# The row maximum of the combine weights, taken from the stored logits or from the reloaded ones

## What is computed

```
x = layernorm(x) ;  se = layernorm(slot_embeds) * scale
logits   = einsum('bnd,esd->bnes', x, se)                    # 2048 rows x 1024 slots
dispatch = softmax(logits, axis=1)                           # over the 1024 rows of a batch
combine  = softmax(logits.reshape(B, N, -1), axis=-1)        # over the 1024 slots of a row
slots = einsum('bnd,bnes->besd', x, dispatch)
gate  = gelu(slots @ Wg + bg) ;  up = slots @ Wu + bu
eout  = (gate * up) @ Wd + bd
out   = einsum('bns,bso->bno', combine, eout)
```

## Time and profile before

| | us |
|---|---|
| median of 3 runs | 626.82 (626.4 to 627.47) |
| the profiled execution | 631.37 |
| its span | 629.6 |
| PE busy | 572.9 (91% of the span) |
| DVE busy | 481.6 (76%) |
| ACT busy | 394.8 (63%) |
| POOL busy | 323.8 (51%) |

### The profile page before, as it was taken

How to read it: one execution, slowest core, us unless ns; L and a number is a source line. 1 busy time by engine, 2 the same in 40 slices (tenths; PEclk the granted TensorE clock), 3 DMA queues, 4 the chain that set the end, 5 groups by cost and what they waited for, 6 DMA issues and landing times.

```text
span 629.6 us, 11863 instructions
## 1 busy us (share of the span) xinstructions
PE 572.9 (91%) x3888; PEld 511.8 (81%) x3888; DVE 481.6 (76%) x1335; ACT 394.8 (63%) x1054; POOL 323.8 (51%) x324
## 2 busy tenths in 40 slices
PE   7697999999979999899888985999879999979998
PEld 3577999999979999899876764988747777769998
DVE  3666877787886978886757998898797999964553
ACT  3747959596864859587734535466465666564563
POOL 5817344444444444443438968666066999830000
PEclk9888999999998999999999999899988999998999
DMA  7800000000020000000002433050057888703552
GB/s 237 219 2 1 2 2 2 1 2 1 10 76 2 2 2 1 2 2 2 1 2 100 169 131 135 1 199 8 1 186 248 266 267 268 269 33 118 176 169 75
DMA packets 34828, 53.36 MB, mean 85 GB/s; under 512 B 6125, under 2 KB 21425, under 8 KB 34769
## 3 DMA queue, kind: packets, MB, share of 16 engines
q1 hardware_dynamic: 34769, 52.61, 24.8%
HBM read 42.12 MB, written 10.49 MB: 84 GB/s over the span
## 4 chain that ended last, share of the span: by engine, by line
PE 50%; DVE 20%; ACT 16%; issue 8%; POOL 5%; DMA 0%; DVEq 0%; SPq 0%; POOLq 0%; ACTq 0%
ACT expo L671 8%; PE ps L1236 8%; PE ps L1367 8%; PE ps L1322 6%; PE ps L1297 5%; PE ps L1344 4%; DVE expo L901 3%; PE ps L1268 3%; DVE qT_low L795 2%; PE ps L1171 2%; PE ps L1356 2%; ACT pT_high L685 2%; PE ps L1190 2%; DVE wkq_low L1016 2%; PE ps L1149 2%
## 5 line engine op out<-in xcount | busy, mean ns | idle before, releaser
L671 ACT ACTIVATE expo<-expo,nmin 128x154 f32<-128x154 f32 x256 | 106.2, 418 | 63.6 <-DVE nmin L901 62.9
L537 POOL TENSOR_TENSOR prob<-expo,prec 128x512 f32<-128x512 f32 x64 | 67.1, 1048 | 113.7 <-DVE prec L912 113.5
L921 DVE TENSOR_TENSOR pT_low<-ps,pT_high 128x512 fp32r<-128x512 f32 (+1 forms) x96 | 54.3, 591 | 19.4 <-ACT pT_high L685 19.2
L901 DVE CUSTOM_DVE_ANT_0 expo<-ps,maskb 128x154 f32<-128x154 f32 x256 | 66.9, 311 | 0.0
L1190 PE MATMUL ps<-kbd,qT_high 128*128 128x308 f32 x256 | 60.7, 322 | 6.0 <-DVE nmin L901 5.7
L598 POOL TENSOR_TENSOR wkq_low<-w_raw,wkq_high 128x1024 fp32r<-128x1024 f32 x16 | 50.8, 3180 | 27.2 <-ACT wkq_high L629 27.2
L685 ACT CAST pT_high<-ps 128x512 fp32r<-128x512 f32 (+1 forms) x96 | 45.9, 512 | 6.1 <-PE ps L1202 5.9
L808 DVE TENSOR_TENSOR w_gu_low<-w_raw,w_gu_high 128x1024 fp32r<-128x1024 f32 x18 | 45.4, 2533 | 4.4 <-ACT w_gu_high L629 4.2
L671 ACT ACTIVATION_READ_ACCUMULATOR expo<-expo,nmin 128x1 f32 x256 | 48.5, 189 | 0.0
L1190 PEld LDWEIGHTS ps<-kbd,qT_high 128*128 128x128 f32 x256 | 40.2, 190 | 9.7 <-DVE nmin L901 9.4
L795 DVE SCALAR_TENSOR_TENSOR qT_low<-ps,bq_c,qT_high 128x256 fp32r<-128x256 f32 x64 | 30.7, 480 | 15.9 <-ACT qT_high L607 15.8
(11 more groups left out here) (215 smaller groups left out, 1824.3 us busy)
## 6 DMA issues: line engine op xcount, KB each, us to landing
logits_dram<-lsb SPq DMA_DIRECT2D x16, 512.0 KB, 2.6
w_raw<-in_L_ffn_Wg_dram SPq DMA_DIRECT2D x16, 512.0 KB, 4.2
w_raw<-in_L_ffn_Wu_dram SPq DMA_DIRECT2D x16, 512.0 KB, 4.5
w_raw<-in_L_ffn_Wd_dram SPq DMA_DIRECT2D x16, 512.0 KB, 4.3
lraw<-logits_dram SPq DMA_DIRECT2D x16, 512.0 KB, 3.5
out_dram<-outb SPq DMA_DIRECT2D x16, 128.0 KB, 1.7
x<-in_x_dram SPq DMA_DIRECT2D x1, 1792.0 KB, 10.1
wraw<-in_L_xattn_Wk_dram SPq DMA_DIRECT2D x2, 512.0 KB, 5.7
```

What stands on the lines that cost most here:

```text
L537: pool.tensor_tensor(prob[:, n % 2, :, heads, :], expo[:, n % 2, pp, :, :, 0:P], prec[:, n % 2, pp].unsqueeze(3).to_broadcast([P, 2, 2, P] ...
L671: ins = act.activation(row, row, ACT.Exp, scale=-1.0, bias=nmin[:, n % 2, pp, j, h:h + 1], accum_out=psums[:, n % 2, pp, j, h:h + 1])
L901: ins = dve.tensor_tensor_reduce(out=expo[:, n % 2, pp, j, h, :], in0=ps[:, s % NS, h * SK:(h + 1) * SK], in1=maskb[:, (2 * (n // QUADS) + ...
L921: dve.tensor_tensor(pT[1][0:rows, n % 2, 2 * t:2 * t + tiles], ps[0:rows, NS + k % NT, 0:tiles * 2 * P].rearrange("p (t n) -> p t n", t=ti ...
```

## The change

The 16 row maxima leave the logits and slots stages. Each is taken in the combine stage instead, by the same DVE instruction, from the reloaded tile `lraw[:, i % 3]` in place of `lsb[:, i]`. DVE now waits for the load, and ACT's exponential waits for the maximum where it waited for the load. `A0` and `A1` stand ahead of `C0` at the end of the experts; `A(i+2)` stands first in step i of the combine stage, ahead of `CT(i+1)`. SP's wait for eight row maxima is gone.

```diff
-A_LATE = 2
-LATER_SLOTS_DVE = {'L': 1, 'A': 4}
+LATER_SLOTS_DVE = {'L': 1}
     for i in range(TILES):                     # logits
         logits += [("x2T", i + 1)] * (i + 1 < TILES) + [("N2", i + 3)] * (i + 3 < TILES) + [("L", i)]
-        logits += [("A", i)] * (i < TILES - A_LATE)
...
-        slots += [("A", TILES - A_LATE + n)] * (n < A_LATE)
...
-    experts += [("C", 0), ("C", 1), ("HT", E - 1), ("EO", E - 2), ("CT", 0, 0), ("CT", 0, 1), ("EO", E - 1)]
+    experts += [("A", 0), ("A", 1), ("C", 0), ("C", 1), ("HT", E - 1), ("EO", E - 2), ("CT", 0, 0), ("CT", 0, 1), ("EO", E - 1)]
...
     for i in range(TILES):                     # combine
+        combine += [("A", i + 2)] * (i + 2 < TILES)
         combine += [("CT", i + 1, 0), ("CT", i + 1, 1)] * (i + 1 < TILES) + [("C", i + 2)] * (i + 2 < TILES)
...
-        sp.wait_ge(amax_ready, TB)
...
             elif ev[0] == "C":                 # ACT
-                act.wait_ge(d_lld[i % 3], 16 * (i // 3 + 1))
+                act.wait_ge(amax_ready, i + 1)
...
             elif ev[0] == "A":                 # DVE
-                dve.tensor_reduce(neg_amax[:, i:i + 1], lsb[:, i], AX, ALU.max, negate=True).then_inc(amax_ready, 1)
+                dve.wait_ge(d_lld[i % 3], 16 * (i // 3 + 1))
+                dve.tensor_reduce(neg_amax[:, i:i + 1], lraw[:, i % 3], AX, ALU.max, negate=True).then_inc(amax_ready, 1)
```

## The result

| | before | changed |
|---|---|---|
| first timing: median (range), 4 runs each | 626.61 (626.33 to 627.47) | 630.72 (629.45 to 631.54) |
| ratio, 95% interval | | 1.0061 (1.0041 to 1.0082) |
| timed again (e5): 29 and 12 runs | 628.13 | 628.75, ratio 1.0008 (0.9989 to 1.0026) |
| timed a third time (e11): 29 and 12 runs | 627.90 | 629.62, ratio 1.0025 (1.0005 to 1.0044) |

So the kernel became slower, by 4.1 us in the first timing and by 1.7 us in the third; the second timing's 0.6 us can't be told from none. I had forecast a gain of 0.15 us. Single executions have to be read with care, since either kernel varies by 5 us from run to run. The mean granted clock of TensorE goes with that only in part.

A forecast was written before the change was run, and what follows sets the result against it. Mostly PE was taken to bound the kernel; -1.0 (logits) + 0 (slots, SP) + 0.55 (end of experts) + 0.3 (combine) = -0.15 us, so 626.82 becomes 626.7 us, range 625.3 to 628.1, forecast chance 0.66.

The forecast's parts named there:

- the wait before tile 10: Logits stage: PE's 0.88 us wait for DVE's low half stays, since at most 0.03 us is won there.
- that before tile 12: Logits stage: PE's 1.08 us wait shrinks by 0.56 to 0.98 us as L10 starts earlier and runs shorter; 0.8 taken.
- the end of POOL's wait: Logits stage: PE's 0.16 us wait for POOL's shift goes as N2.14 starts earlier; 0.2 us taken with small change.
- Rivals 1 and 4: Logits stage: 1, PE regains all waits, 625.5 us, chance 0.11; 4, POOL replaces DVE, nothing won, 627.7 us, 0.08.
- my 2.12 us: Logits stage: sum of PE's three waits that matter, the most PE could win by sparing DVE.
- SP's wait and the slots stage: Removing SP's wait for eight maxima, and A14 and A15 from the slots stage, wins nothing.
- The end of the experts: A0 before the combine stage makes ACT's first exponential 0.55 us late, all added to the end; A1 is hidden.
- Rival 2: End of the experts: ACT's table load stands behind the wait for A0, 1.28 us slower, 628.0 us; chance 0.08.
- The combine stage: Reductions A2 to A15 fit unless a load takes over 4.1 us; one does, costing 0.3 us, bounds 0 and 1.6.
- the one over PE, three steps long: Combine stage loop, scaling of CO(0) to CO(3): 7.24 us plus landing, in 11.22 us; binds from a 4.0 us landing.
- rival 3: Combine stage: store, load, reduction, exponential and transposes become the bound, all landings 4.4 us, costing 1.6, 628.0 us; chance 0.07.
- the margin of 0.38 us: Combine stage: tile 4 can be transposed at 578.74, PE wants it at 579.12, so loads may take 4.1 us.

The follow-up runs named there:

- e5: The changed kernel timed again beside the kernel before: 628.75 against 628.13 us, ratio 1.0008.
- e11: The changed kernel timed a third time, on another chip: 629.62 us against 627.90 for the kernel before, ratio 1.0025.
- e1: The kernel before, unchanged, run for a second profile: 625.9 us.
- e2: Kernel before with all 16 row maxima removed and nothing in their place, the exponential taking exp(0 * logit + 0): 626.26 us against 627.61, ratio 0.9983.
- e3: Changed kernel with the 16 old reductions put back as well, into a tile nobody reads: 630.09 us against 627.61 for the kernel before, ratio 1.0044.
- e10: Changed kernel with C(i+2) and CO(i) exchanged in the combine stage: 627.67 us, ratio 0.9999 to the kernel before.
- e8: Kernel before with STORE_LAG 2, so loads start one step later: 662.54 us.
- e9: Kernel before with STORE_LAG 2 and C(i+2) and CO(i) exchanged in the combine stage: 647.83 us.
- e4: Changed kernel with STORE_LAG 4 in place of 3, so loads are issued earlier: 625.87 us against 627.61 for the kernel before, ratio 0.9966.
- e6: Kernel before with STORE_LAG 4: 627.57 us against 628.13, ratio 0.9996.
- e7: Changed kernel with STORE_LAG 4 and A0 taken ahead of GU15 on DVE: 626.76 us against 628.13 for the kernel before, ratio 0.9984.
- e12: Changed kernel with STORE_LAG 4 and A0 ahead of GU15, timed on another chip: 626.89 us against 627.90 for the kernel before, ratio 0.9964.

## Why the prediction was wrong

**The logits stage** went as worked out, step by step: the wait before tile 10 stayed, that before tile 12 went from 1.08 down to 0.11 us (I had about 0.3), POOL's went away. Won: 1.3 us where I took 1.0. Both parts of the 0.56 to 0.98 us that I had for tile 12 came, and the end of POOL's wait gave 0.3 us where I took 0.2 (from the matmuls of tile 12 to the transposes of tile 14 PE now takes 3.76 us, 4.07 before). Rivals 1 and 4 fall. A fourth wait, which my 2.12 us left out, is the same in both kernels: 1.59 us for POOL's shift early in the stage (at 338.16 before). That reductions never held POOL up, the row beside which I set the Trainium skill's rule on the shared ports ("SBUF — State Buffer", section "Who interferes with whom"), agrees: POOL won nothing but the earlier start of `N2.14`, and was busy for 53.2 us of the stage before and for 53.4 after. **SP's wait and the slots stage** were worth nothing, as said (SP's first load after that place is issued at 412.29, again with the end of POOL's eighth shift, 409.86 + 2.40 = 412.26).

**The end of the experts** cost 0.64 us where I had 0.55, and the table load lay ahead of the wait. Rival 2 falls. All of that was small: the terms outside the combine stage came to -0.6 us where I had -0.45.

**The combine stage** is where it failed. The step was: "Of the twelve loads from 4 on, one took longer than 4.1: load 11, with 4.4 us. It costs 0.3 us once." The mechanism and the threshold were right (waits are the landing less 4.0), the term was mis-sized by five to ten times: 1.6 to 2.9 us against 0.3. Two things made it up.
1. The number of late loads. I counted them in one execution, in which nobody waited for them. In the changed kernel there are 4 with 4.2 us or more (4.2, 4.4, 4.6, 4.8), in e5 3 (4.2, 4.3, 4.4), in e11 3 (4.4, 4.4, 4.9). In e1, the second profile of before, there is again only one, and in e2, with the same combine stage but for the exponential, there are 2.
2. The price of one. After each wait PE's transposes take 0.22 us longer; I had priced the wait alone.

The late loads are not scattered, which I had overlooked. In the eight profiles with a `STORE_LAG` of 3 they fall on the same four places. Issue to landing, us:

| load | 4 | 8 | 11 | 15 | longest of the other eight |
|---|---|---|---|---|---|
| before, e1, e2 | 3.7, 3.6, 3.5 | 3.8, 3.9, 4.1 | 4.4, 4.4, 4.5 | 3.6, 3.9, 4.4 | 3.7, 3.8, 3.9 |
| changed, e5, e11 | 4.2, 3.7, 3.9 | 4.6, 4.4, 4.4 | 4.4, 4.2, 4.4 | 4.8, 4.3, 4.9 | 3.9, 3.9, 3.9 |
| e3, e10 | 4.1, 4.2 | 3.9, 4.0 | 5.1, 4.4 | 5.0, 4.5 | 4.0, 4.0 |

Load 11, the one that I counted, is late in all eight. Loads 4, 8 and 15 landed 0.4, 0.3 and 0.7 us later on average in the five profiles with the reductions in the combine stage than in the three without. So part of the miss may lie in what the change does to the landings themselves, and not in which execution I had read. That it does, and how, no run shows.

**A loop that I had not seen** belongs to the account, though it cost nothing here. I looked for the one over PE, three steps long, and found 4.0 us as the landing from which it binds. A shorter one goes over DVE's order: reciprocal of tile i+2, scaling and store of tile i, load i+4. e8 and e9 show it in the kernel before. In the changed kernel it is two steps long. Its DVE and SP rows behind load 4:
```profile
576.59 0.17 DVE L1057 RECIPROCAL crec<-csum 128x1 f32<-128x1 f32 x1
576.89 0.48 DVE L1073 SCALAR_TENSOR_TENSOR outb<-ps,crec,x 128x256 f32<-128x256 f32 x1
```
```profile
569.82 1.34 SPq L464 DMA_DIRECT2D lraw<-logits_dram  x1
...
577.78 0.43 SPq L464 DMA_DIRECT2D lraw<-logits_dram  x1
```
From load 4 to load 6 are 7.96 us, the landing of 4.22 and 3.74 us more, against two steps of 7.48. So from a landing of 3.74 us the next load but one is late, and 3.8 us is the changed kernel's median. But load 6 then landed in 3.35 us and PE did not wait for it. None of the four loads that PE waited for had been made late in this way: loads 8 and 15 were issued 7.46 and 7.47 us after the load but one ahead, load 11 8.25 us after it, in which PE's stop for tile 8 lies. e10 agrees. Were all landings at 4.4 us, this loop would bind before the one that I priced: (4.4 + 3.74) / 2 = 4.07 us a step, some 4 us in all by this estimate, and not rival 3's 1.6.

Rival 3 named the mechanism that decided, late loads that PE ends up waiting for behind the reduction, with a price of 1.6 us for all twelve. I gave it 0.07 since the margin of 0.38 us looked like one; the landings that I had read reached 4.4 already. The stage did not become bound by it throughout, as the rival had it: three or four of twelve loads made nearly all of the loss.

The first timing's 4.1 us is more than these terms give (1.0 to 2.3 us), and the rest of it stays open beyond the small samples named under e5 and e11. Of the two larger timings 1.7 us agrees with the terms, and 0.6 with its interval.

## What to carry to other kernels

A step put between a load and its first reader takes its length from the load's slack at once: price it by the landings of several executions, load by load, not by the median of one; late ones can come back at the same places, as load 11 did here eight times. Ask how early the load could be issued, which here was one constant. When an instruction starts to wait, write down what is queued behind it on its engine down to the next load, and work out each such loop's time per step, since it takes over when that exceeds the step of the stage, as in e8. Before two executions are compared, their stages and granted clocks have to be, since either kernel varied by more than the change was worth.

## What the runs showed of the hardware

The issue of a load on SP's queue took 0.43 us in most cases and 0.6 to 2.0 us in one to five of the twelve in each profile, and its landing was mostly late with it (1.65 us and 4.8 us for load 15 of the changed kernel). Some loads landed late without it (load 8: 0.43 and 4.6 us). The long issues stand at fixed places: among loads 4, 8, 11 and 15 with a `STORE_LAG` of 3 (but for load 5 in e3, 0.67 us), and among 5, 9 and 12 with 4 (e4, e6, e7, e12), where all landings over 4.05 us are too. What makes an issue long was not tried. The Trainium skill, "DMA: Bandwidth & Descriptors", section "Latency and other measured facts", puts most of a transfer's fixed cost on the access to the memory, 0.2 us on average and up to 2 us at high load; no run here separates that from the rest.
